# The ninth round of a graph-network kernel takes its two matrices straight from bytes of a packed word

## The reference, cut to what matters

```python
def _L0_gnn_ref(x, adj, W1, b1, W2, b2):
    mask = (adj > 0.0)
    h = relu((x @ W1a)[:, :, None, :] + (x[:, :, None, :] - x[:, None, :, :]) @ W1b + b1)   # b, node, neighbour, 192
    hm = einsum('bjkh,bjk->bjh', h, mask)
    return hm @ W2 + sum(mask, -1)[..., None] * b2
x = layernorm(x + L0(x, adj, ...))
x = layernorm(x + L1(x, adj, ...))
```

## Time and profile before

| | |
|---|---|
| median of 3 runs | 900.94 us (900.2 to 903.97) |
| span of the profiled execution | 904.5 us |
| VectorE busy | 823.7 us, 91%, 945 instructions |
| TensorE matmuls busy | 823.8 us, 91%, 10240 instructions |
| ScalarE busy | 616.5 us, 68% |
| GpSimd busy | 454.9 us, 50% |
| first B1 on VectorE / B1 of turn 31 | 48.65 us / 823.26 us |

### The profile page before, as it was taken

The page is one execution under the profiler, slowest core; times in us unless marked ns, Lnnn a source line. Parts: engine busy times, 40 slices in busy tenths (PEclk is TensorE's granted clock), DMA queues, the critical chain, the costliest instruction groups (busy, mean ns, idle before and its releaser), DMA issues.

```text
span 904.5 us, 25621 instructions
## 1 busy us (share of the span) xinstructions
PE 823.8 (91%) x10240; PEld 565.4 (63%) x10240; DVE 823.7 (91%) x945; ACT 616.5 (68%) x1799; POOL 454.9 (50%) x533
## 2 busy tenths in 40 slices
PE   3778889999999999999999999999999999999973
PEld 2445657666676756666675766667675766666652
DVE  6789999999999999999999999999999999998842
ACT  4534556686876868686786868687786868677641
POOL 4413233564736465473736456473746556353741
PEclk9889999999999999999999999999999999999976
DMA  3331211312130222313131131213122131121000
GB/s 125 88 74 31 71 49 48 83 48 78 49 95 19 61 82 48 93 35 93 48 81 34 49 95 48 78 47 96 27 72 64 49 94 43 48 49 31 1 12 25
DMA packets 31562, 53.34 MB, mean 59 GB/s; under 512 B 8272, under 2 KB 17104, under 8 KB 31440
## 3 DMA queue, kind: packets, MB, share of 16 engines
q1 hardware_dynamic: 31440, 51.67, 21.5%
HBM read 13.90 MB, written 4.19 MB: 20 GB/s over the span
## 4 chain that ended last, share of the span: by engine, by line
PE 63%; issue 17%; DVE 9%; ACT 5%; POOL 4%; DMA 1%; SPq 1%; POOLq 0%; DVEq 0%
PE PS L839 16%; PE PS L848 12%; DVE AC L1177 5%; PE PS L916 3%; POOL AC L1732 2%; PE PS L904 2%; PE PS L825 2%; PE PS L656 2%; PE PS L667 2%; PE PS L926 2%; DVE AC L1157 1%; PE PS L607 1%; PE PS L802 1%; PE PS L616 1%; PE PS L923 1%
## 5 line engine op out<-in xcount | busy, mean ns | idle before, releaser
L1157 DVE SCALAR_TENSOR_TENSOR AC<-PS,AC 128x1152 f32<-128x1152 f32 (+1 forms) x279 | 339.8, 1218 | 19.1 <-PE PS L848 9.6
L1177 DVE SCALAR_TENSOR_TENSOR AC<-PS,AC 128x1152 f32<-128x1152 f32 (+1 forms) x279 | 339.9, 1218 | 15.6 <-PE PS L839 15.2
L839 PE MATMUL PS<-DM,VA 128*128 128x192 fp8e5 (+1 forms) x1152 | 134.6, 240 | 18.1 <-DVE AC L1157 11.5
L839 PE MATMUL PS<-DM,VB 128*128 128x192 fp8e5 (+1 forms) x1152 | 136.5, 242 | 0.8 <-DVE AC L1174 0.8
L1732 POOL TENSOR_TENSOR AC<-AC,NNB 128x512 f32<-128x512 f32 x64 | 66.7, 1061 | 113.0 <-DVE DM L1124 80.9
L848 PE MATMUL PS<-DM,VB 128*64 128x192 fp8e5 (+1 forms) x1152 | 96.5, 246 | 24.3 <-DVE AC L1177 20.8
L839 PEld LDWEIGHTS PS<-DM,VA 128*128 128x128 f16 x1152 | 85.6, 100 | 47.3 <-DVE AC L1157 39.1
L839 PEld LDWEIGHTS PS<-DM,VB 128*128 128x128 f16 x1152 | 76.1, 98 | 38.4 <-DVE AC L1174 1.5
L848 PE MATMUL PS<-DM,VA 128*64 128x192 fp8e5 (+1 forms) x1152 | 98.0, 250 | 0.1
L848 PEld LDWEIGHTS PS<-DM,VB 128*64 128x64 f16 x1152 | 46.5, 109 | 72.7 <-issue 45.8
L1685 POOL TENSOR_SCALAR MT<-AT 128x1024 bf16<-128x1024 f32 x15 | 42.0, 2797 | 60.0 <-DVE DM L1124 52.3
(11 more groups left out here) (263 smaller groups left out, 2001.8 us busy)
## 6 DMA issues: line engine op xcount, KB each, us to landing
CW<-WM SPq DMA_DIRECT2D x128, 160.0 KB, 2.8
AT<-in_adjt SPq DMA_DIRECT2D x16, 512.0 KB, 4.9
VA<-VN SPq DMA_DIRECT2D x64, 96.0 KB, 2.2
VB<-VN SPq DMA_DIRECT2D x64, 96.0 KB, 2.2
XN<-in_xn SPq DMA_DIRECT2D x16, 256.0 KB, 4.9
out<-YO SPq DMA_DIRECT2D x15, 256.0 KB, 2.9
cs<-in_cst SPq DMA_DIRECT2D x1, 545.5 KB, 3.5
out<-YO SPq DMA_DIRECT2D x2, 128.0 KB, 1.7
```

Of the source, the lines that this page charges most:

```text
L839: last = e.matmul(PS[:, b + i % 2, 256 * (i // 2) + cols.start:256 * (i // 2) + cols.stop], lhs[:, GRAPH[i], 0:128], d[:, i, :], start=Fal ...
L1157: e.scalar_tensor_tensor(dst, tiles(PS[:, b:b + 3, :])[:, :, cols], 0.0, dst, ALU.max, ALU.add).then_inc(s["sx"], 1)
L1177: e.scalar_tensor_tensor(dst, tiles(PS[:, b:b + 3, :])[:, :, cols], 0.0, dst, ALU.max, ALU.add).then_inc(s["sy"], 1)
```

## The change

The constant that is shifted for the 512 words of `second` is 0xC040 in place of 7, and the shift is 8 times (9 - rank) in place of 2 times (rank - 8). So the low byte of a word is 0x40 (+2) where the rank is 9, which is the switch matrix, and the high byte is 0xC0 (-2) for rank 9 and 0x40 (+2) for rank 8, which is the matrix of round 9. TensorE reads CW itself, one byte of two, for both. `dgen` with m = 4 and `switch` are gone from all engines, with the tiles DM[4] and SW and their codes in the order. TensorE waits for the DMA that fills CW, and SP's `words` waits also for round B9 of quartet q-3, because that is now CW's last reader.

```diff
-RD = 5
+RD = 4
 ORDER = (
-    ("2ps3ee", "t", "", "pp", "", "ed", "4dre", "t", "rtpp", "tc", "erdeee", "", "pdr", "p", "e", "pp", "rp", "w", "0e1"),
-    ("d2sp3", "pp", "", "t", "dpe", "t", "pe", "4pcttn", "n", "lpd", "d", "p", "d", "d0", "d", "p", "rdddp", "", "wp1"),
+    ("2ps3ee", "t", "", "pp", "", "ed", "dre", "t", "rtpp", "tc", "erdeee", "", "pdr", "p", "e", "pp", "rp", "", "0e1"),
+    ("d2sp3", "pp", "", "t", "dpe", "t", "pe", "pcttn", "n", "lpd", "d", "p", "d", "d0", "d", "p", "rdddp", "", "p1"),
 )
...
+            def lasts(q, h, b):
+                pe.wait_ge(s[f"dW{q % 3}"], 64 * (q // 3 + 1))
+                w = CW[(q + h) % 3][:, h, second].bitcast(F8).rearrange("p (i n b) -> p i n b", i=4, b=2)
+                return w[:, :, :, b]
+
             def steps(t, h, n):
-                pe.wait_ge(s["dd"], RD * t + (n - 1) % 4 + 1 if n < 9 else RD * t + 5)
                 if n == 9:
-                    return DM[4][:, h, 0:512].bitcast(F8).rearrange("p (i n b) -> p i n b", i=4, b=2)[:, :, :, 1], nat
+                    return lasts(t - h, h, 1), nat
+                pe.wait_ge(s["dd"], RD * t + (n - 1) % 4 + 1)
...
                 if n == 1:
-                    pe.wait_ge(s["sw"], q + 1)
                     pe.wait_ge(s["sx"], 9 * q + 9)
-                    wide(q, VA[q % 3], SW[:], nat)
-                    paired(q, VA[q % 3], SW[:], nat)
+                    leave = lasts(q, 0, 0)
+                    wide(q, VA[q % 3], leave, nat)
+                    paired(q, VA[q % 3], leave, nat)
...
-                e.activation(am[:, second].rearrange("p (i n) -> p i n", i=4), src, ACT.Copy, scale=2.0,
-                             bias=-272.0).then_inc(s["am"], 1)
+                e.activation(am[:, second].rearrange("p (i n) -> p i n", i=4), src, ACT.Copy, scale=-8.0,
+                             bias=8.0 * (128 + C0)).then_inc(s["am"], 1)
...
-                e.memset(c7[:], 7)
+                e.memset(c7[:, first], 7)
+                e.memset(c7[:, second], 0xC040)
...
                 sy.wait_ge(s["dd"], RD * (q - 1))
+                sy.wait_ge(s["gy"], 9 * (q - 2))
```

More of the change, by code:

```diff
@@ L61 @@
 ORDER = (
-    ("2ps3ee", "t", "", "pp", "", "ed", "4dre", "t", "rtpp", "tc", "erdeee", "", "pdr", "p", "e", "pp", "rp", "w", "0e1"),
-    ("d2sp3", "pp", "", "t", "dpe", "t", "pe", "4pcttn", "n", "lpd", "d", "p", "d", "d0", "d", "p", "rdddp", "", "wp1"),
+    ("2ps3ee", "t", "", "pp", "", "ed", "dre", "t", "rtpp", "tc", "erdeee", "", "pdr", "p", "e", "pp", "rp", "", "0e1"),
+    ("d2sp3", "pp", "", "t", "dpe", "t", "pe", "pcttn", "n", "lpd", "d", "p", "d", "d0", "d", "p", "rdddp", "", "p1"),
 )
-FIRST = ("s2pp", "p", "p3p4p", "", "rpp", "", "r", "p", "r", "", "", "pr", "rp", "", "", "", "", "0", "crw1")
+FIRST = ("s2pp", "p", "p3pp", "", "rpp", "", "r", "p", "r", "", "", "pr", "rp", "", "", "", "", "0", "cr1")
 LAST = (
-    ("2std", "t3", "w4d", "t", "t", "nned", "d", "dn", "d", "ddn", "", "d", "d", "n", "d", "d", "nd0", "1ne", ""),
-    ("2ted", "t", "", "edd3e", "", "te", "et", "ed", "ddddn", "ndedde", "n", "edd4dn", "nn", "e", "n", "d", "", "", "n"),
+    ("2std", "t3", "d", "t", "t", "nned", "d", "dn", "d", "ddn", "", "d", "d", "n", "d", "d", "nd0", "1ne", ""),
+    ("2ted", "t", "", "edd3e", "", "te", "et", "ed", "ddddn", "ndedde", "n", "edddn", "nn", "e", "n", "d", "", "", "n"),
 )
@@ L259, in build @@
         DM = [sb(f"DM{i}", [128, 2, 768], U16) for i in range(RD)]
-        SW = sb("SW", [128, 4, 128], BF16)
         AC = [sb(f"AC{i}", [128, 3, 512]) for i in range(3)]
@@ L541, in between @@
                             do("dgen", t + 1, int(c))
-                        elif c in "234":
+                        elif c in "23":
                             do("dgen", t, int(c))
@@ L545, in between @@
                             do("seeds", t)
-                        elif c == "w":
-                            do("switch", t)
                         elif c == "c":
@@ L1121, in dgen @@
                 halves = slice(0 if t < NQ else 1, 2 if t else 1)
[L1122 to L1134, removed]
+                e.tensor_scalar(DM[m][:, halves], CW[t % 3][:, halves, first], 6 - 2 * m, 0xC0C0, ALU.logical_shift_left,
+                                ALU.bitwise_and).then_inc(s["dd"], 1)
             def round_a(q, n):
@@ L1275, in vector_main @@
             follow(main_order, {"consts": consts, "mask": mask, "count": count, "off": off, "words": words,
-                                "dgen": dgen, "switch": switch, "round_a": round_a, "round_b": round_b,
+                                "dgen": dgen, "round_a": round_a, "round_b": round_b,
                                 "wide_w": wide_w, "fold": fold, "s_ov": s_ov, "bias": bias, "flag": flag, "fsum": fsum,
```

## The result

Measured beside each other, the changed kernel took 904.5 us (median of 20 executions, 901.72 to 907.41) and the kernel before 901.67 us; ratio 1.0022, 95% interval 1.0011 to 1.0032. Two later comparisons of the same two kernels gave 902.41 us, 1.0005 (0.9988 to 1.0021), and 903.29 us, 1.0011 (0.9994 to 1.0028). So the change makes no difference by the bound of 0.5%. It tends to slower (one of the three intervals leaves 1 out), where 2.5 us of gain, 898.4 us, had been forecast.

The account below looks back on a forecast made before the run. VectorE and TensorE were taken to bound the kernel alternately, stretch by stretch. Even-turn switches 1.8, odd-turn switches 0.6 and last turns 0.1 made 2.5 us, from 900.94 to 898.4 us; range 892.0 to 904.5.

Parts of the forecast that it names:

- Parts 1 and 2: Round 9's dgen in even and odd turns: removal gains 0, since TensorE's work covers it (odd turns 0.03 at most).
- Part 3: Switch of the odd turn, before A9: A1 starts 0 to 0.08 us earlier, taken as 0.05; 12 turns give 0.6 us.
- Part 4: Switch before the even turn: GpSimd's product of the seeds shortens, A1 starts 0.15 us earlier; 12 times, 1.8 us.
- TensorE's earlier switch matmuls: Before the even turn, TensorE gets its switch matmuls at once: under 0.1 us, and no more of A1.
- TensorE's waits for the DMA of CW are met turns earlier; it has one wait less: TensorE's waits on CW's DMA, listed among what is moved or added; no cost was put on them.
- The third rival: v's DMAs, issued by SP, come late to A1 of even turns: 9.3 us slower, 910.2 us; chance 0.12.
- Random over the turns: Argument against v coming late to A1: long DMA issues on SP fall randomly over the turns.

Follow-up runs that it names:

- f2: Changed kernel with v's VA DMAs issued before VB's, 32 memsets each heading VectorE's and GpSimd's streams, CW wait moved to B5: 898.95 us, ratio 0.9964.
- d2: Changed kernel with v's two DMAs for VA issued ahead of those for VB, a semaphore for each pair: ratio 0.9994 against the kernel before.
- e3: Repeat of the changed kernel with v's DMAs re-ordered (VA before VB): ratio 0.9991 against the kernel before, 667.6 us in turns 4 to 29.
- c4: Changed kernel with one more TensorE wait, for a dgen of the next turn, between switch matmuls and B1; A1 waited 0.6 to 1.1 us in turns 24 to 30.

## Why the prediction was wrong

By its own steps:

- *Parts 1 and 2, the dgens:* the cover was as read; VectorE's gain of 0.3 to 0.4 us at these places is lost again at the next round, as said. But the price of 0 left out what the part does to TensorE's queue (below).
- *Part 3, 0.05:* VectorE's A1 comes 1.65 us after B1 in turn 19 and 1.69 before. Right, though some 0.03 of it is lost again by A7.
- *Part 4, 0.15:* the thread was right and its size off. The first dgen took over the wait (1.06 us at 482.63), GpSimd's product fell from 2.12 to the 1.97 us forecast, but it also starts 0.06 us later counted from B1; so A1 came 0.09 earlier (1.92 us after B1 in place of 2.01), not 0.15.

```profile
482.63 1.06 DVE L1125 TENSOR_SCALAR DM<-CW 128x1536 uint16<-128x1536 uint16 x1
...
484.54 1.97 POOL L1725 TENSOR_TENSOR AC<-AC,NNB 128x512 f32<-128x512 f32 x2 [1.27 <-ACT AC L1508]
```

- *TensorE's earlier switch matmuls, "under 0.1, and no more of A1":* they give 0.04 us at the end of odd turns, which the sum didn't count. With it the switch alone reaches 0.18 of the 0.20 us per pair.
- *"TensorE's waits for the DMA of CW are met turns earlier; it has one wait less": the step that failed.* It put TensorE's waits at nothing, because it counted them and did not look at their places. First, CW's DMA was long done, but TensorE had not asked before: its wait now stands at A9, on the thread, as a second one, and costs 0.08 us in every even turn, 1.0 us in turns 4 to 29. Second, the wait that went had held TensorE's queue, and with it the fetch of its instructions, behind v's DMAs: 2 to 3 us more of waits at A1. A third loss, 0.65 us at turns 6 and 14, depends on the count of instructions and stands in no term of the sum either.
- *The third rival* named the right wait with the wrong trigger. It looked to SP's instruction stream, and it is TensorE's that is fetched. The long issue on SP that it had seen is real, but it is the second way, and the kernel before had it as well; SP's issues ahead of turn 20 are of the ordinary 0.47 and 0.60 us. "Random over the turns" was wrong too, and its price of 9.3 us counted all even turns where five or six are hit.

The sum for turns 4 to 29 of the first profile: even turns 13 x -0.03 = -0.4, odd turns 13 x -0.07 = -0.9, turns 6 and 14 +0.65, A1's waits +2.1, together +1.45 us; measured 670.3 - 668.8 = +1.6. The same three causes taken away give f2, 2.7 us below before in these turns, 1.2 of which are waits at A1 that the kernel before had there.

What stays open: turn 30 takes 26.5 to 27.0 us, or 29.5 to 30.1 with 6.8 us of half clock (1.2 GHz) that begin between 800 and 805. Five of the eleven profiles with the whole change have it, none of the other six, which is too few to tell. The changed kernel's mean clock over 44 executions is no lower (0.9817, before 0.9805), so I take it for no part of the result; but d2 with e3 ran at 0.9785, and 1.0 us of their -1.4 in the table is the correction for that. What calls the stretch up was not tried.

## What to carry to other kernels

A wait that costs next to nothing is not free to remove or to move. The one for the switch, removed, had kept TensorE's instruction fetches behind a DMA that A1 needs soon. The one for CW's DMA, which always passes at once, costs 0.08 us where it is the second wait of an instruction on the thread, and nothing at an instruction that has slack. So look at which instruction will carry a new wait, and at what stands close to the next 16 KB of the busiest instruction stream. Where a transfer is met without slack, give its first half a semaphore of its own (here 2.7 to 3.2 us in turns 4 to 29). Differences of 1 to 3 us in 900 are told only at equal granted clock, or from turns at full clock.

## What was not expected of the hardware

- A 16 KB fetch of TensorE's instructions takes 0.9 to 1.7 us and delays a part of a DMA issued beside it by up to 1.6 us. With the fetch 1.4 to 1.7 us ahead of A1 the wait was 0.5 to 1.25 us (none in turn 4), at 3.2 to 3.6 us up to 1.0, at 0.5 to 1.1 us none or 0.15, but 1.10 once (turn 26 of c4).
- A DMA issue on SP beside such a fetch took 0.99 to 2.14 us in place of 0.47 to 0.61.
- With two waits in place of one at TensorE's A9 it was 0.146 us from A8's end to the first matmul, against 0.057.
- The block between VectorE and GpSimd passes to whatever stands next: the switch's 0.80 us became a dgen's 1.06 for 0.55 beside an idle GpSimd. The Trainium skill (SBUF — State Buffer, section "Who interferes with whom") says that whichever of the two issues first gets the shared ports for its whole instruction, and that the other blocks fully. The trace agrees in kind only: the dgen ended 0.42 us after GpSimd's instruction beside it (483.27), less than its own 0.55, so by these rows it had not been kept from starting altogether. Ends on GpSimd are rough in a profile, though.
- TensorE reads one byte of two from CW at the pace of DM: 0.055 us from matmul to matmul of 128 columns in both.
